# A macaron block in split half precision: narrow stationary operands widened to 128 columns and rows, and the norms' shift taken from one operand

## The reference, cut to what matters

```python
x = x + 0.5 * ffn(layernorm(x))
x = x + attn(layernorm(x))
x = x + 0.5 * ffn(layernorm(x))

# attn: 16 heads of 64
q, k = rmsnorm(x @ Wq), rmsnorm(x @ Wk)
gate = softplus(einsum('bthd,hd->bht', k, u / norm(u)) / sqrt(64))
bias = -dist[None, None] * omega_eff[None, :, None, None] * gate[:, :, None, :]
scores = einsum('bihd,bjhd->bhij', q, k) / sqrt(64) + bias      # causal
y = softmax(scores) @ v ;  out = y @ Wproj

# ffn: hidden 512, with W1 and W2 each changed per batch by outer products of the first tokens
h = gelu(x @ (W1 + scale * m1).T + b1) ;  out = h @ (W2 + scale * m2).T + b2
```

## Time and profile before

| what | value |
|---|---|
| time, median of 3 runs | 792.8 us (791.22 to 794.23) |
| the profiled execution: its own time | 796.93 us |
| its span, first to last instruction | 794.9 us |
| busy: PE, DVE, ACT, POOL | 759.8 (96%), 671.7 (84%), 654.7 (82%), 640.6 (81%) |
| granted TensorE clock, mean | 0.989 of full |
| chain that ended last | PE 67%, ACT 17%, DVE 5%, issue 5%, POOL 2%, DMA 2% |
| DMA | 97298 packets, 77.12 MB; 71662 packets under 512 B |

### The profile page before, as it was taken

One profiled execution on the slowest core, in us unless ns is written; L12 is line 12 of the kernel. 1 busy time (PEld: TensorE's weight loads), 2 busy tenths in 40 slices (PEclk: granted clock), 3 DMA queues, 4 the chain that ended last, 5 costly groups with the idle time before them and its releaser, 6 DMA issues.

```text
span 794.9 us, 25364 instructions
## 1 busy us (share of the span) xinstructions
PE 759.8 (96%) x9445; PEld 536.0 (67%) x9445; DVE 671.7 (84%) x2098; ACT 654.7 (82%) x1420; POOL 640.6 (81%) x751
## 2 busy tenths in 40 slices
PE   5789999899999999999999989999999999999988
PEld 2446767577667776677667766677766776677765
DVE  8779878978988888988979789888888889899955
ACT  6659877878998889897998879988898979986762
POOL 5427868878988989889889878889898898987690
PEclk9799999999999999999999999999999999999999
DMA  7071625555173633636162641736326361538520
GB/s 196 9 161 41 125 53 126 79 122 109 29 162 68 148 70 69 148 80 152 29 145 58 134 96 28 163 68 134 84 63 155 73 158 29 126 79 156 89 41 28
DMA packets 97298, 77.12 MB, mean 97 GB/s; under 512 B 71662, under 2 KB 84080, under 8 KB 97176
## 3 DMA queue, kind: packets, MB, share of 16 engines
q1 hardware_dynamic: 96696, 73.92, 44.3%
q10 hardware_dynamic: 480, 1.57, 0.8%
HBM read 4.74 MB, written 2.10 MB: 9 GB/s over the span
## 4 chain that ended last, share of the span: by engine, by line
PE 67%; ACT 17%; DVE 5%; issue 5%; POOL 2%; DMA 2%; SPq 1%; POOLq 0%; ACTq 0%; DVEq 0%
PE ps L1048 12%; PE ps L1050 11%; PE ps L1049 11%; PE ps L1197 7%; PE ps L1198 7%; PE ps L1170 7%; PE ps L1152 4%; ACT qkn L979 3%; PE ps L1199 3%; ACT pt L1008 3%; ACT qkn L934 2%; ACT sq L933 2%; DVE masked L1508 2%; ACT hid L919 1%; ACT v_buf L994 1%
## 5 line engine op out<-in xcount | busy, mean ns | idle before, releaser
L813 POOL TENSOR_TENSOR pt_l<-pt 128x512 f16<-128x512 f32 x368 | 319.3, 897 | 69.8 <-ACT pt L1008 69.6
L1508 DVE CUSTOM_DVE_ANT_0 masked<-ps,causal_row 128x512 f16<-128x512 f32 x448 | 192.2, 486 | 16.1 <-PE ps L1170 14.6
L1008 ACT ACTIVATE pt<-ps 128x512 f32<-128x512 f32 (+1 forms) x384 | 175.2, 530 | 29.5 <-PE ps L1199 17.5
L839 POOL TENSOR_TENSOR qkn<-qkn,rs 128x512 f32<-128x512 f32 x128 | 130.5, 1047 | 29.1 <-ACT rs L945 29.0
L1197 PE MATMUL ps<-qk 128*128 128x512 f16 (+3 forms) x512 | 146.9, 300 | 0.0
L1198 PE MATMUL ps<-qk 128*128 128x512 f16 (+3 forms) x512 | 146.5, 299 | 0.0
L1048 PE MATMUL ps<-v_buf,pt 128*128 128x65 f16 x1280 | 129.8, 194 | 0.9 <-POOL pt_l L813 0.7
L1049 PE MATMUL ps<-v_buf,pt 128*128 128x65 f16 x1280 | 129.8, 193 | 0.0
L1050 PE MATMUL ps<-v_buf,pt_l 128*128 128x65 f16 x1280 | 129.5, 193 | 0.0
L1048 PEld LDWEIGHTS ps<-v_buf,pt 128*128 128x128 bf16 x1280 | 118.0, 98 | 7.2 <-issue 2.5
L1049 PEld LDWEIGHTS ps<-v_buf,pt 128*128 128x128 bf16 x1280 | 117.6, 98 | 3.4
(11 more groups left out here) (198 smaller groups left out, 2003.9 us busy)
## 6 DMA issues: line engine op xcount, KB each, us to landing
qk<-qkn SPq DMA_DIRECT2D x186, 256.0 KB, 4.2
x_in<-in_L_attn_x SPq DMA_DIRECT2D x8, 256.0 KB, 3.2
out<-x_out SPq DMA_DIRECT2D x8, 256.0 KB, 2.5
qk<-qkn ACTq DMA_DIRECT2D x6, 256.0 KB, 5.0
qk<-qk SPq DMA_DIRECT2D x1, 1024.0 KB, 8.2
qk<-gtt SPq DMA_DIRECT2D x64, 8.0 KB
qk<-nmt SPq DMA_DIRECT2D x64, 2.0 KB
y_hl<-ytt SPq DMA_TRANSPOSE x63, 3.1
```

The lines of the kernel that those rows point to most:

```text
L813: g.tensor_tensor(pt_l[:, h % 2, c], pt[:, h % 2, c], pt_h[:, h % 2, c], ALU.subtract).then_inc(s_pt_l, 1)
L839: g.tensor_tensor(qk, qk, r.unsqueeze(4).broadcast_to([P, 2, 2, 2, D]), ALU.mult).then_inc(s_qkn, 1)
L1008: a.activation(pt[:, h % 2, c], ps[:, j, 0:width], ACT.Exp).then_inc(s_exp, 1)
L1508: ins = d.tensor_tensor_reduce(masked[:, part.unit(s, i)[0], col:col + (ib + 1) * P], part.bank(s, i)[:, col:col + (ib + 1) * P], causal_r ...
```

## The change

- `maxima` becomes 128 columns per quad, in the order (parity of the head, pair, token block), of which 16 are written and the rest hold zero; one transpose with a stationary operand 128x128 takes the place of four with 128x4. ACT's copy is 16x128 in place of 4x512, and the two DMAs per quad read 8 rows of 128 in place of 2 rows of 512.
- `gate`, `zero` and `gt` are laid out anew so that (head, row kind, pair, token block) gives 128 contiguous columns; one transpose 128x128 takes the place of four of 128x32. DVE's copy is 128x128 in place of 32x512; each DMA reads 32 rows of 128 in place of 8 rows of 512. POOL's multiplication writes with another stride.
- `ones`, `b2rows`, `z_hl` and `sel` get 128 rows. The number of matmuls of "m" and "out" and their columns stay.
- DVE clears `maxima` and the lower halves of `z_hl` and `sel` at the start (three more memsets).
- `rstd` is written over the variance in `mv`, and `shift` is one reduction (product, negated) along the last axis of `mv`.

```diff
-        b2rows = sb("b2rows", [LO_ROW + 1, TB, C], F16)
-        ones = sb("ones", [LO_ROW + 1, P], F16)
+        b2rows = sb("b2rows", [P, TB, C], F16)
+        ones = sb("ones", [P, P], F16)
...
-        rstd = {n: sb(f"rstd_{n}", [P, TB]) for n in NORMS}
+        rstd = {n: mv[n][:, :, 1] for n in NORMS}
...
-        z_hl = sb("z_hl", [2 * ROWS, C], F16)
-        sel = sb("sel", [2 * ROWS, 2 * FB, P], F16)
+        z_hl = sb("z_hl", [P, C], F16)
+        sel = sb("sel", [P, 2 * FB, P], F16)
...
-        gate = sb("gate", [P, TB, 2, HH])
+        gate = sb("gate", [P, QH, 2, 2, TB])
...
-        gt = sb("gt", [P, TB, 4, HH], F16)
-        gtt = sb("gtt", [4 * HH, T], F16)
-        maxima = sb("maxima", [P, TB, H], F16)
+        gt = sb("gt", [P, QH, 4, 2, TB], F16)
+        gtt = sb("gtt", [P, P], F16)
+        maxima = sb("maxima", [P, H // QH, P], F16)
...
-        nmt = sb("nmt", [QH, T], F16)
+        nmt = sb("nmt", [QH * TB, P], F16)
...
+        def max_column(h, ib):
+            at = h % 2 * 2 * TB + h % QH // 2 * TB + ib
+            return maxima[:, h // QH, at:at + 1]
...
-                                 gtt[qd % 2 * 2 + n::4, :]).then_inc(s_gates[qd % 2], 16)
+                                 gtt[(qd % 2 * 2 + n) * 8 * TB:(qd % 2 * 2 + n + 1) * 8 * TB, :]).then_inc(s_gates[qd % 2], 16)
...
-                    sp.dma_start(qk1[MROW:MROW + 1, qd, n, 1, :, :], nmt[n::2, :]).then_inc(s_mrow, 16)
+                    sp.dma_start(qk1[MROW:MROW + 1, qd, n, 1, :, :].rearrange("o i (t c) -> o (i t) c", c=P), nmt[n * 2 * TB:(n + 1) * 2 * TB, :]).then_inc(s_mrow, 16)
...
-                g.tensor_tensor(gate[:, :, :, :], softplus[:, :, :].unsqueeze(2).broadcast_to([P, TB, 2, HH]),
-                                omj[:, :, :, hf * HH:(hf + 1) * HH], ALU.mult).then_inc(s_gate, 1)
+                g.tensor_tensor(gate[:, :, :, :, :].rearrange("p s r i t -> p t r i s"),
+                                softplus[:, :, :].rearrange("p t (i s) -> p t i s", s=QH).unsqueeze(2).broadcast_to([P, TB, 2, 2, QH]),
+                                omj[:, :, :, hf * HH:(hf + 1) * HH].rearrange("p t r (i s) -> p t r i s", s=QH),
+                                ALU.mult).then_inc(s_gate, 1)
...
-                part.taken_by(a.activation(nmt[:, :], part.bank(s)[0:QH, :].bitcast(F16)[:, 0:T], ACT.Copy, scale=-1.0), s)
+                part.taken_by(a.activation(nmt[:, :], part.bank(s)[0:QH * TB, :].bitcast(F16)[:, 0:P], ACT.Copy, scale=-1.0), s)
...
-                for t in range(TB):
-                    mm = pe.transpose(part.bank(s)[0:4 * HH, :].bitcast(F16)[:, t * P:(t + 1) * P],
-                                      gt[:, t, :, :].rearrange("p r h -> p (r h)"), ident16[:, :])
-                part.filled_by(mm, s)
+                part.filled_by(pe.transpose(part.bank(s).bitcast(F16)[:, 0:P],
+                                            gt[:, :, :, :, :].rearrange("p s r i t -> p (s r i t)"), ident16[:, :]), s)
...
-                for t in range(TB):
-                    mm = pe.transpose(part.bank(s)[0:QH, :].bitcast(F16)[:, t * P:(t + 1) * P],
-                                      maxima[:, t, qd * QH:(qd + 1) * QH], ident16[:, :])
-                part.filled_by(mm, s)
+                part.filled_by(pe.transpose(part.bank(s).bitcast(F16)[:, 0:P], maxima[:, qd, :], ident16[:, :]), s)
...
+            d.memset(maxima[:, :, :], 0.0)
+            d.memset(z_hl[2 * ROWS:P, :], 0.0)
+            d.memset(sel[2 * ROWS:P, :, :], 0.0)
...
-                d.scalar_tensor_tensor(shift[n][:, :], mv[n][:, :, 0], -1.0, rstd[n][:, :], ALU.mult,
-                                       ALU.mult).then_inc(s_shift[n], 1)
+                d.tensor_reduce(shift[n][:, :], mv[n][:, :, :], AX.X, ALU.mult, negate=True).then_inc(s_shift[n], 1)
...
-                part.taken_by(d.tensor_copy(gtt[:, :], part.bank(s)[0:4 * HH, :].bitcast(F16)[:, 0:T]), s)
+                part.taken_by(d.tensor_copy(gtt[:, :], part.bank(s).bitcast(F16)[:, 0:P]), s)
...
-                        top = maxima[:, ib, h:h + 1]
+                        top = max_column(h, ib)
```

More of the change, by code:

```diff
@@ L420, in macaron @@
         softplus = sb("softplus", [P, TB, HH])
-        gate = sb("gate", [P, TB, 2, HH])
+        gate = sb("gate", [P, QH, 2, 2, TB])
         omr = sb("omr", [P, H])
         omj = sb("omj", [P, TB, 2, H])
-        zero = sb("zero", [P, TB, 2, HH])
-        gt = sb("gt", [P, TB, 4, HH], F16)
-        gtt = sb("gtt", [4 * HH, T], F16)
-        maxima = sb("maxima", [P, TB, H], F16)
+        zero = sb("zero", [P, QH, 2, 2, TB])
+        gt = sb("gt", [P, QH, 4, 2, TB], F16)
+        gtt = sb("gtt", [P, P], F16)
+        maxima = sb("maxima", [P, H // QH, P], F16)
         masked = sb("masked", [P, len(RING), T], F16)
-        nmt = sb("nmt", [QH, T], F16)
+        nmt = sb("nmt", [QH * TB, P], F16)
         pt = sb("pt", [P, 2, SCOLS])
@@ L783, in _ @@
                             pattern=[[1, P]], channel_multiplier=-1).then_inc(s_const, 1)
-            g.memset(zero[:, :, :, :], 0.0).then_inc(s_zero, 1)
+            g.memset(zero[:, :, :, :, :], 0.0).then_inc(s_zero, 1)
             pool.wait_ge(s_zero, 1)
@@ L848, in gates @@
                 pool.wait_ge(s_softplus, g2)
-                g.tensor_tensor(gate[:, :, :, :], softplus[:, :, :].unsqueeze(2).broadcast_to([P, TB, 2, HH]),
-                                omj[:, :, :, hf * HH:(hf + 1) * HH], ALU.mult).then_inc(s_gate, 1)
+                g.tensor_tensor(gate[:, :, :, :, :].rearrange("p s r i t -> p t r i s"),
+                                softplus[:, :, :].rearrange("p t (i s) -> p t i s", s=QH).unsqueeze(2).broadcast_to([P, TB, 2, 2, QH]),
+                                omj[:, :, :, hf * HH:(hf + 1) * HH].rearrange("p t r (i s) -> p t r i s", s=QH),
+                                ALU.mult).then_inc(s_gate, 1)
                 pool.wait_ge(s_gate, g2)
-                g.tensor_tensor(gt[:, :, 0::2, :], gate[:, :, :, :], zero[:, :, :, :], ALU.add).then_inc(s_gt_h, 1)
+                g.tensor_tensor(gt[:, :, 0::2, :, :], gate[:, :, :, :, :], zero[:, :, :, :, :], ALU.add).then_inc(s_gt_h, 1)
                 pool.wait_ge(s_gt_h, g2)
-                g.tensor_tensor(gt[:, :, 1::2, :], gate[:, :, :, :], gt[:, :, 0::2, :], ALU.subtract).then_inc(s_gt, 1)
+                g.tensor_tensor(gt[:, :, 1::2, :, :], gate[:, :, :, :, :], gt[:, :, 0::2, :, :], ALU.subtract).then_inc(s_gt, 1)
             def value_weights_lo(part, s, b):
@@ L950, in inverse_root @@
                 act.wait_ge(s_lnv[n], b + 1)
-                a.activation(rstd[n][:, :], lnv[n][:, :], ACT.Exp, scale=-0.5).then_inc(s_rstd[n], 1)
+                a.activation(rstd[n], lnv[n][:, :], ACT.Exp, scale=-0.5).then_inc(s_rstd[n], 1)
             def normalize(part, s, b, n):
```

## The result

| | before | after |
|---|---|---|
| median of the runs, us | 792.59 (4 runs, 791.22 to 794.23) | 784.23 (4 runs, 783.62 to 785.34) |
| after / before, 95% interval | | 0.9882 (0.985 to 0.9914) |
| profiled execution: its own time, us | 796.9 | 783.62 |
| profiled execution: span, us | 794.9 | 781.3 |
| granted clock, mean | 0.989 | 0.989 |

The change takes 8.4 us, about half of the 17.9 that were forecast. 784.2 lies inside the range of 766 to 785, at its upper end. The spans of the two profiled executions differ by 13.6 us. That is more than the medians do, since the one before stands 4.3 us over its median (it holds the long shift of the earlier trace rows) and the one after 0.6 under.

What follows compares the result with a forecast made beforehand. PE was taken as the bound, busy 91.45 of 91.90 us per steady batch. 16.8 (PE stages) + 2.1 (ACT's copy) - 1.0 (memsets) = 17.9 us off 792.8 gave 774.9, forecast 775 us; range 766 to 785.

Steps and rivals of the forecast that it cites:

- The gap is a weight load of another shape: PE, beside four narrow-operand stages: the differently shaped load is not slid under the running matmul; about 0.10 us in, 0.09 out.
- The rival that only the passes would fall: PE: the gap has another cause, so only removed passes count, 6.0 us; 7.1 in all, 786 us; chance 0.11.
- Of these stages the chain holds 57 pieces ... 16.8 us: PE: 24 "nm", 11 "gr", 9 "m", 13 "out" on the chain at full price, 16.8 us; bounds 6.0 and 23.4.
- Others close up: PSUM banks between PE and ACT or DVE: PE waits for banks, half of the 16.8 lost, 783 us; chance 0.14.
- PE does not wait, it works: PE, steady batch: busy 91.45 of 91.90 us, so shorter pitches shorten the kernel wherever PE is the chain.
- ACT's copy, 2.1 us: ACT's copy of the maxima: 578 to 278 ns, seven copies in the chain, 2.1 us saved, between 1.4 and 9.6.
- The shift, 0 in the median: Norms' shift on DVE: the one-operand form is never held; 0 taken in the median, up to 3.2 us.
- The memsets, 1.0 us lost: Three DVE memsets in the lead, ahead of the first norm: 1.0 us lost, 1.5 if all shows.
- The weight loads' 4.5 us: PE's weight loads: by the skill page's rule, widening 48 stages gives back some 4.5 us if nothing hid it.
- The gate rows' DMA: Gate rows' DMAs into stage "a": shorter pieces priced at nothing, with a slack of 1.4 us.
- The rival by which it would end slower: Stage "a" waits for late gate rows in 256 B pieces, landing 6.5 us in place of 2.4: 797 us; chance 0.03.
- further 3.2: Profiled execution only: one long hold of the norms' shift goes, a batch of 95.10 us against 91.90, 3.2 us.

Runs made afterwards that it cites:

- the lighter ACT: Changed kernel with only ACT's squares cut to 8 elements per head, DVE still adding 64: 771.74 us, ratio 0.972 to the kernel before.
- lighter readers: ACT's squares and DVE's sums cut from 64 to 8 per head: kernel before with the one-operand shift 784.95 us, changed kernel 768.78 us.

## Why the prediction was right or wrong

**The gap is a weight load of another shape: right.** It went at all four stages, from the columns' side and from the rows', but for 0.05 us behind some, and came back with 16 columns. The rival that only the passes would fall is out as a cause, though its 786 lies close to the time that came.

**"Of these stages the chain holds 57 pieces ... 16.8 us": this is the step that failed.** The price per stage was right. That each stage in the chain counts its full price was not. The rows of "m" and "out" count for 2.6 to 5.1 of 6.1 us. The maxima and the gates count for little. From the rows with the shift to the whole change is 3.1 us by the ratios (0.9921 and 0.9882, of two sets), and 4.9 us within one set (788.56 to the 783.64 of the changed kernel with its memsets moved), for 32 x 0.36 + 16 x 0.36 = 17.3 us of PE and ACT's shorter copy on top. The steady batches, 90.96 and 90.39, give 0.57 of 2.16 us. Behind most "nm" and "gr" comes, within a few us, a stage that needs a bank from ACT or DVE, and PE arrives there earlier and waits. The rival "Others close up" put half of the 16.8 at risk and gave 783; it is what came. So the time fell inside the range by the rival's mechanism and not by that of the forecast, whose own 770 to 780 it missed. The argument against the rival, that their load was 8 us under PE's, compared sums over a batch. Banks are handed back at single points, and at some of these ACT had no slack, although it idles 10 us of each batch elsewhere.

**"PE does not wait, it works": right for the kernel before, and not enough.** PE was busy 91.45 of 91.90. Such a row says that PE sets the pace now. It does not say how far it can be shortened before the next engine sets it: here by 0.1 to 0.3 us at a time.

**ACT's copy, 2.1 us: right in size (255 ns, for 278 forecast), not seen in the time.** It is part of the maxima, which brought 0.2 alone. The chain of the changed kernel holds none of the 32 copies, where it held seven before. Whether the copy is worth anything by itself was not tried.

**The shift, 0 in the median: right alone, mis-sized in the change.** Alone it brings 1.1, not clear of noise. In the change its absence costs 29 us, about five holds at 5.9 us of a batch each (96.25 for 90.39). I took the hold for "an accident of phase" and asked only whether it would go. The other edits move that phase, and with the rows' edit alone the accident comes in five shifts of seven. The slower outcome that this kernel was closest to was not late gate rows, but an edit that is right in itself and made without the shift. How few hundredths decide is in no row that I quoted: the earlier trace rows is the one shift at 0.30, and the others of norm c that met a train's head stood at 0.35. "Most of the 21 are short" was a misreading too: nine took 0.15 to 0.16 us, twelve were held, eleven of them for 0.27 to 0.98.

**The memsets, 1.0 us lost: not settled.** They take 0.87 us on DVE, and the run with them moved cannot tell what of it shows.

**The weight loads' 4.5 us.** This estimate stands beside the sum and not in it. It took the price of 4-column loads for all 48 stages. By its own working, four loads of 32 columns are as long as one of 128, so only the 32 "nm" count: 32 x (107 - 13) ns = 3.0 us.

**The gate rows' DMA: right.** PE's waits name it only in the lead (1.6 us in all, 1.5 before). The rival by which it would end slower is refuted, and with it the case for it that 256 B pieces had. An issue of the maxima's rows takes 666 ns for 601, one of the gate rows 720 for 726. The gate product on POOL costs 328 ns for 321.

**The sum.** Of 17.9: 16.8 became about 8; the copy's 2.1 and the memsets' 1.0 are not seen in the time. The "about 8" holds what the shift and the copy gave as well. The profiled execution's further 3.2 was there: its stretch with the hold took 23.96 us, and the same stretch takes 20.42 after, 3.5 us. The spans' 13.6 is the medians' 8.4, the 4.3 by which the profiled execution before stands over its median (3.5 of it the hold, the rest scatter), the 0.6 by which the one after stands under its own, and 0.3 by which time and span differ more after than before.

**What stays open**: why 0.30 or 0.35 us decides between a hold of six instructions and of one. Whether ACT takes the time back through the banks it frees late or also through what else it delivers is not separated: the lighter ACT speeds up both, and POOL too waits for it (60 us in 46 waits for the exponentials, L1014). And what it would bring in full if the squaring (L939) read the copy in SBUF, so that the bank came free after L940 alone, which was not tried.

## What to carry to other kernels

A stage's place in the chain tells what the engine did, not what a cut there brings: look for the next stage that needs a buffer back, and ask what that buffer's reader does in the time freed. A cheap way to ask is to lighten the reader and repeat the comparison: here the same cut was worth 7 to 8 us, and 16.2 with lighter readers. And a small VectorE instruction with two SBUF operands on the path beside a train of GpSimd work is worth rewriting to one operand before other edits are judged, since they may be judged by where it happens to start.

## What the runs showed of the hardware

- A stationary operand narrower than the array, in columns (4, 16, 32) or in rows (64, 33), between full ones costs some 0.10 us on the way in and 0.09 on the way out, each time: 0.31 and 0.15 with 16 columns, 0.22 and 0.05 with 128. Beside stages of 96 rows no such gap was seen (the 96x512 stages start 0.05 to 0.06 behind a pass of 128 columns, as full ones do).
- A 128x4 instruction of VectorE with two SBUF operands was held 4.9 to 5.05 us when it began 0.14 to 0.30 us behind the first of six back-to-back GpSimd subtractions (11 of 11), and 0.70 us when it began 0.35 to 0.36 behind it (19 of 19). Where it began beside a later subtraction, it ended with that one in 33 cases of 36 (held for at most 0.98 us) and one later in two. With one operand it took 0.15 to 0.165 us in all 189 places of nine runs, and nine of these began 0.16 to 0.26 us behind the first of six subtractions.
- Where such holds left PE idle for 3.0 to 5.4 us of a batch, batch after batch, the granted clock over that batch was 0.96 to 0.98 in place of 1.00. In the one batch of the kernel before with a hold, PE was idle for 3.1 us and the clock stayed at 1.00.
